# A graph transformer kernel on one core: ScalarE makes the keys' mask addends that GpSimd made, and GpSimd masks three steps of four instead of two

## What is computed

```
qkv = layer_norm(x, g1, be1) @ w_qkv          # 4096 x 3 x 8 heads x 16
scores = einsum("nhd,mhd->hnm", q, k) * 16 ** -0.5
scores = where(adj != 0, scores, -inf)
attn = softmax(scores, axis=-1)
x = x + einsum("hnm,mhd->nhd", attn, v) @ w_proj + b_proj
x = x + gelu(layer_norm(x, g2, be2) @ w1 + b1) @ w2 + b2
```

## Time and profile before

| | us |
|---|---|
| median of 3 runs | 3656.32 |
| lowest, highest | 3652.48, 3665.82 |
| the profiled execution | 3654.05 |
| its span, first to last instruction | 3652.3 |
| layer 0 attention, step 0's exponential to the barrier | 203.6 to 1722 |
| even passes 2 to 12 of layer 0, each | 97.2 to 97.8 |
| odd passes 1 to 13 of layer 0, each | 93.6 to 95.4 |

### The profile page before, as it was taken

One profiled execution on the slowest core, in us unless ns is written; L12 is line 12 of the kernel. 1 busy time (PEld: TensorE's weight loads), 2 busy tenths in 40 slices (PEclk: granted clock), 3 DMA queues, 4 the chain that ended last, 5 costly groups with the idle time before them and its releaser, 6 DMA issues.

```text
span 3652.3 us, 68569 instructions
## 1 busy us (share of the span) xinstructions
PE 3436.8 (94%) x22572; PEld 1388.6 (38%) x22572; DVE 2968.7 (81%) x8997; ACT 2337.5 (64%) x2596; POOL 2489.9 (68%) x1476
## 2 busy tenths in 40 slices
PE   6999999999999999998869999999999999999988
PEld 3443333333333333332634433333333333333326
DVE  6889888888988898870568998999999989999604
ACT  4348686877777777866341466666666666666753
POOL 1057878787878787878110587787888787878870
PEclk9589999999999999999896799999999999999989
DMA  3578787878786869683232546454555555555432
GB/s 131 179 225 261 239 267 226 274 227 281 218 285 210 290 211 295 200 254 94 78 113 84 176 140 187 141 175 154 171 163 169 162 164 165 161 171 157 145 96 67
DMA packets 480351, 676.31 MB, mean 185 GB/s; under 512 B 51552, under 2 KB 272864, under 8 KB 475616
## 3 DMA queue, kind: packets, MB, share of 16 engines
q1 hardware_dynamic: 479568, 671.83, 59.2%
q10 hardware_dynamic: 432, 0.10, 0.0%
HBM read 508.14 MB, written 165.68 MB: 184 GB/s over the span
## 4 chain that ended last, share of the span: by engine, by line
PE 41%; POOL 36%; issue 13%; DVE 7%; DMA 2%; POOLq 1%; ACT 1%; DVEq 0%; SPq 0%; ACTq 0%
POOL arena L929 36%; PE PS L463 13%; PE PS L443 10%; PE PS L476 7%; PE PS L470 7%; DVE spill L806 5%; PE PS L416 3%; POOLq L907 1%; PE PS L449 1%; DVE arena L766 0%; PE PS L586 0%; DMA arena<-out_dram 0%; PE PS L407 0%; ACT o_sb L679 0%; DMA mask<-in_adj_t 0%
## 5 line engine op out<-in xcount | busy, mean ns | idle before, releaser
L806 DVE CUSTOM_DVE_ANT_0 spill<-PS,mask_n 128x512 bf16<-128x512 f32 x4096 | 2635.8, 688 | 278.0 <-PE PS L443 177.4
L671 ACT ACTIVATE arena<-PS 128x1024 f32<-128x1024 f32 x2048 | 1991.8, 1022 | 911.3 <-PE PS L476 870.4
L929 POOL TENSOR_TENSOR arena<-arena,mask 128x1024 int32<-128x1024 int32 x896 | 2136.8, 2385 | 638.0 <-ACT arena L671 633.0
L443 PE MATMUL PS<-k_t,q_t 48*128 48x512 f32 x4096 | 1288.3, 547 | 60.1 <-DVE pmax L806 40.2
L463 PE MATMUL PS<-arena,v_sb 128*32 128x512 f32 x8192 | 1099.4, 609 | 41.6 <-ACT o_sb L679 37.5
L470 PE MATMUL PS<-q_t,k_t 50*128 50x512 f32 x4096 | 934.3, 466 | 0.3 <-POOL arena L919 0.2
L443 PEld LDWEIGHTS PS<-k_t,q_t 48*128 48x128 f32 x4096 | 545.6, 194 | 1022.9 <-DVE pmax L806 911.8
L476 PE MATMUL PS<-arena,idb 64*128 64x512 bf16 x4312 | 841.8, 391 | 0.0
L470 PEld LDWEIGHTS PS<-q_t,k_t 50*128 50x128 f32 x4096 | 400.1, 188 | 199.6 <-ACT arena L671 121.7
L476 PEld LDWEIGHTS PS<-arena,idb 64*128 64x128 bf16 x4312 | 208.9, 95 | 465.5 <-issue 343.3
L806 DVE DVE_READ_ACCUMULATOR2_ANT pmax<- 128x1 f32 x4096 | 340.0, 83 | 0.0
(11 more groups left out here) (54 smaller groups left out, 979.9 us busy)
## 6 DMA issues: line engine op xcount, KB each, us to landing
mask<-m_dram SPq DMA_DIRECT2D x768, 256.0 KB, 2.7
mask_n<-mn_dram SPq DMA_DIRECT2D x768, 128.0 KB, 2.7
adj_in<-in_adj SPq DMA_DIRECT2D x256, 256.0 KB, 3.9
mask<-in_adj_t SPq DMA_DIRECT2D x256, 256.0 KB, 4.0
m_dram<-mask SPq DMA_DIRECT2D x256, 256.0 KB, 3.6
mn_dram<-mask_n SPq DMA_DIRECT2D x256, 128.0 KB, 3.8
mt_dram<-arena SPq DMA_DIRECT2D x256, 128.0 KB, 3.5
arena<-mt_dram SPq DMA_DIRECT2D x256, 128.0 KB, 2.8
```

Of the source, the lines that this page charges most:

```text
L443: pe.matmul(bank, q_t[r0:r0 + KROWS, gb % Q_SLOTS, pair, q * P:(q + 1) * P], k_t[r0:r0 + KROWS, pair, mb * TILE:(mb + 1) * TILE], start=Tr ...
L671: nc.scalar.activation(p_buf[:, t % P_SLOTS, 2 * half:2 * half + 2, :], ps_b[:, 2 * half:2 * half + 2, :], ACT.Exp, scale=SCALE).then_inc( ...
L806: dve.tensor_tensor_reduce(spill[:, j % A_BANKS, :], ps_a[:, j % A_BANKS, :], mask_n[:, v % N_SLOTS, :], 1.0, LOWEST, ALU.subtract, ALU.ma ...
L929: pool.tensor_tensor(p, p, m, ALU.mult).then_inc(p_masked, 1)
```

## The change

POOL's `make_masks` keeps only the 0/1 words. The addends are now made by ACT, in a new function `mask_keys(t)`, from POOL's words: `exp(69 + MASKED * word)`, written to `mask_t` as bf16. The value is positive, so the identity matrix `idb` becomes its negative. ACT's stream has `mask_keys(t + 2)` right behind the second exponential of step t, and ahead of any `mask_rows` there. And `pooled` in layer 0's even passes now holds for three steps of four (all but t % 4 == 0) instead of two.

```
         def pooled(L, t):
 
-            return L > 0 or t // MT % 2 == 1 or t % 2 == 1
+            return L > 0 or t // MT % 2 == 1 or t % 4 > 0
...
+            def mask_keys(t):
+                nb, s, slot = t // (2 * MT), t % MT, t % M_SLOTS
+                act.wait_ge(mask01_made, MADE[t + 1])
+                if nb > 0:
+                    act.wait_ge(b_scored, 2 * (t - MT) + 2)
+                    if s == 0:
+                        act.wait_ge(mt_stored, nb * MT * 16)
+                nc.scalar.activation(mask_t[:, s, :], mask01[:, slot, :].bitcast(U32), ACT.Exp,
+                                     bias=far[:], scale=MASKED).then_inc(t_made, 1)
...
+                for t in range(2):
+                    if made(L, t):
+                        mask_keys(t)
                 for t in range(STEPS):
                     exp_pair(L, t, 0)
                     if t > LAG and t % MT == LAG:
                         keep_o(L, t // MT - 1)
                     exp_pair(L, t, 1)
-                    while made < len(visits) and visit_step(visits[made]) - 3 < t + 1:
-                        mask_rows(visits[made])
-                        made += 1
+                    if t + 2 < STEPS and made(L, t + 2):
+                        mask_keys(t + 2)
+                    while at < len(visits) and visit_step(visits[at]) - 3 < t + 1:
+                        mask_rows(visits[at])
+                        at += 1
                 keep_o(L, 2 * NB - 1)
...
             def make_masks(t):
-                nb, s, slot = t // (2 * MT), t % MT, t % M_SLOTS
+                slot = t % M_SLOTS
                 m = mask01[:, slot, :]
                 pool.wait_ge(adjt_loaded[slot], fills(0, t) * 16)
                 pool.tensor_scalar(m, m.bitcast(U32), 1.0, 0.0, ALU.min, ALU.max).then_inc(mask01_made, 1)
-                if nb > 0:
-                    pool.wait_ge(b_scored, 2 * (t - MT) + 2)
-                    if s == 0:
-                        pool.wait_ge(mt_stored, nb * MT * 16)
-                pool.wait_ge(mask01_made, MADE[t + 1])
-                pool.tensor_scalar(mask_t[:, s, :], m, -MASKED, MASKED, ALU.mult, ALU.add).then_inc(t_made, 1)
...
-    ident = give("ident", np.eye(P, dtype=ml_dtypes.bfloat16))
+    ident = give("ident", -np.eye(P, dtype=ml_dtypes.bfloat16))
```

More of the change, by code:

```diff
@@ L689, in mask_rows @@
                                      bias=far[:], scale=MASKED).then_inc(n_made, 1)
+            def mask_keys(t):
[7 more added lines that the diff above has]
+                                     bias=far[:], scale=MASKED).then_inc(t_made, 1)
             def attend(L):
                 visits = [v for v in range(NV) if rows_made(L, v)]
-                made = 0
-                while made < len(visits) and visit_step(visits[made]) < 3:
-                    mask_rows(visits[made])
-                    made += 1
+                at = 0
+                while at < len(visits) and visit_step(visits[at]) < 3:
+                    mask_rows(visits[at])
[3 more added lines that the diff above has]
+                        mask_keys(t)
                 for t in range(STEPS):
```

## The result

| | before | after |
|---|---|---|
| median, us (5 runs each on one chip) | 3656.38 | 3691.47 |
| lowest, highest | 3652.48, 3665.82 | 3678.69, 3696.44 |
| the profiled execution, its span | 3654.05, 3652.3 | 3685.58, 3683.7 |
| odd passes 1 to 13 of layer 0 | 93.6 to 95.4 | 93.5 to 95.5 |
| even passes 2 to 12 of layer 0 | 97.2 to 97.8 | 101.5 to 104.4 |

A forecast was written before the change was run, and what follows sets the result against it. A ring between ACT and PE was taken as the bound. Terms 6.4 + 2.1 - 2.2 + 7.0 + 9.6 = +22.9 us gave 3679 us beside 3656.32, range 3656 to 3704.

The forecast's parts named there:

- The ring: Middle of even passes: ACT's addends wait for POOL's words behind products, 0.16 us lost per four-step cycle, +6.4 us.
- the gain of 0.27 a step: Even passes: each step moved to POOL saves 0.27 us, 64 steps 17.3 us if nothing else were late.
- Starts of passes: Pass starts: ACT's wait for words, 7 x 0.3 = +2.1 us, against saved steps worth -2.2 us.
- the saved step: First steps of a pass: ACT's wait hides in PE's long gaps; 8 x -0.27 = -2.2 us.
- Row masks: Pass ends: next pass's first row masks stand behind ACT's addends, delaying exponentials of steps 25 and 27; +7.0 us.
- Late loads: Mid-pass: queries' 1 MB load makes POOL's words late and ACT now waits; 7 x 1.37 = +9.6 us.
- The turn: Pass end after step 27: PE's long gap of 2.08 us hides the remaining delay; costed at nothing.
- Rival 4: Even passes: PE, held more often, drops to its 1.2 GHz clock; adds 12 us, 3691 in all; 12%.
- SP's queue: SP's store waits for ACT's addends with the next words' load behind it; costed at nothing, some 2 us in hand.
- rival 3: SP falls behind, so POOL gets its words late in every cycle; +34 us on the forecast, 3713; 10%.
- Rival 1: Even passes: the whole gain of 17.3 us comes, as POOL's words arrive in time; 3639 us; 8%.
- The signs: Profile after: L698 idle over 10 us, even passes 99 to 101 us, four steps 11.7 to 11.9, products 3.05 apart.

The follow-up runs named there:

- e1: The changed kernel with POOL's words made three steps ahead instead of two, their loads unmoved: 3710.03 us, ratio 1.0142 to the kernel before.
- e7: Changed kernel with queries' load issued earlier, turn as four reductions, words made three steps ahead and their loads one step earlier: 3597.86 us, ratio 0.9828.
- e9: The changed kernel, but step 26 of even passes not masked by POOL (8 products fewer): 3668.67 us, ratio 1.0021.
- e2: The changed kernel with SP's 1 MB load of the next queries issued 20 steps earlier, in an odd pass: 3681.73 us, ratio 1.0054.
- e3: The changed kernel with POOL masking two steps of four as before, so only ACT's addends are new: 3671.03 us, ratio 1.0031.
- e5: The kernel before with DVE's four small turn operations written as four reductions, one drain fewer: 3611.85 us, ratio 0.9865.

## Why the prediction was right, and where it failed

- **The ring.** Right in kind: L698 waits for POOL in three steps of four, and more than half of the gain of 0.27 a step is gone (with the words early, e1 and e7, four steps take 11.33); e1 shows that the words' place in POOL's stream does it. Its size and sign were off: -0.12 a cycle for +0.16. The term at fault is product and words together, 3.05 from the pitch of two unlike operations in the earlier trace rows (2.35 + 0.70). The rows of after have 415.32 to 415.89, 0.57, for words followed by a product, so 2.93. Over the two further steps in which POOL is behind this takes 0.24 off, where the cycle was 0.27 too long; the rest are small terms of both signs, as the latency from the words to ACT (415.96 - 415.93 = 0.03 for 0.08), the addend to the exponential (0.63 for 0.61) and the exponentials (1.92 for 1.94).
- **Starts of passes.** Both terms were too large, and by luck they cancel. The gap before a pass's first step grew by 0.1, from 0.88 to 0.98, and not by 0.3; and the saved step, -0.27 in each pass, isn't there: the gaps before steps 1 to 6 are the same in both traces in the seven later passes, 1.3, 1.4 and 1.7 first, set by the mask turn. The first pass's 4.3 us are the clock's earlier rise, which no term had and the change didn't cause.
- **Row masks.** 1.62 and 1.57 at steps 25 and 27 against the forecast 1.70 and 1.6: +7.0 was forecast, +6.9 measured for these gaps. The part called hidden shows at step 30 (1.72 for 1.11), and is paid for by a shorter turn where that is undisturbed (1.57 + 1.40 in e9, 1.10 + 2.1 or so before). In e1, where the words are there early, the same row masks cost nothing (1.11 and 1.11), so this term hangs on the ring.
- **Late loads.** The mechanism was right, and e2 shows the 1 MB load as its cause. The term was 1.37 a pass from pass 2's load; it measured 1.1 to 2.9, in all 12.6 for 9.6, and the stretches at 1.2 GHz behind it came on top, 17.2 in the table. The load comes later than in the trace it was read from. SP issues the words of step 84 at 443.08 us, 0.55 after the start of step 80's exponentials where it was 0.08, because its store of the addends now waits for ACT; in the other six passes it is 0.55 to 1.52 where it was 0.06 to 0.26. And in pass 2 POOL starts 9.65 us after that issue, before 8.69, for which no run shows the cause; in the other passes that time is at most 0.1 longer than before.
- **The turn: the step that failed.** "After step 27 PE's turn leaves a long gap [...], which hides the rest". The turn was taken as slack at no cost, and what DVE does in it wasn't looked at, although the diff makes step 26, whose product runs then, a POOL step. The sign was in the trace of before: a cast of 1.00 us in odd passes and of some 0.18 in even ones. The row measured +17.9 for 0, and e9 puts the price at 20 us, more than the whole shortfall of 12: the cycle and the first steps, 12 us better than forecast in the table, hid a part of it.
- **The clock: an alternative that was an addition.** Rival 4 was given 12% and a time of its own, 3691, the measured one to the microsecond. This is luck in part: the rest of the forecast was to hold beside it, and it didn't. The rival should have hung on the waits that the sum itself had put at PE: who forecasts 1.4 us more idle time in seven places, behind which PE is full of work, has to price the slower microseconds behind them as well. The five executions of after agree: the shortest, 3678.69 us, has a mean granted clock of 0.951, the longest, 3696.44, of 0.947.
- **SP's queue.** Its waits for the addends rose from 50.2 us to 123.2, which the prediction cost at nothing. POOL's waits for loads fell from 29 to 20, so rival 3 did not happen; but the 0.5 us and more by which the loads are issued later is part of the late load's price. The nearest relative of rival 3 is e1, where POOL ran ahead of the loads.
- **Rival 1** failed as argued. The Trainium skill's rule of taking work off GpSimd (Perfetto Trace Analysis, Optimizing GPSIMD Operations) did not hold in e3, which does only that (1.0031), and came true only in e7, behind four other edits.
- **The signs.** L698's idle time, the gap of over 2 us in mid-pass and the unchanged odd passes came. Even passes of 101.5 to 104.4 us for 99 to 101, four steps in 11.50 for 11.7 to 11.9 and products 2.93 apart for 3.05 did not.

The table's parts don't split exactly into waits and clock. Cast and subtraction make 8 x 1.0 + 2.2 = 10 us, the late gaps 12.6, the row masks 6.9; eleven more stretches in even passes at 1.5 us would make 16, and the cycle and first steps -8, of which 4.3 are the clock in pass 0. The sum is 38 for 34.7 measured; that an idle turn hides a part of each is likely, and not shown.

## What to carry to other kernels

When a change gives GpSimd more steps, list the small VectorE operations on the critical path that will now run beside a GpSimd operation, and look in the trace for the same line at two durations: a wait of this kind stands inside the row, with no idle time before it. When an engine gets a wait for another engine's product, ask in every queue how early its inputs are there, and move the producer and its loads by the same step: here the producer alone made the kernel slower (e1, 1.0142), and with its loads moved too, beside the queries' load moved and the turn as reductions, it was faster (e7). And count what follows a new idle time of PE, not only the idle time. Last, compare traces stretch by stretch also where nothing should differ: 4.3 us of this comparison were the clock's rise at the start.

## What the runs showed of the hardware that was not expected

- A VectorE cast or copy of 128x16 fp32 elements takes 0.18 us alone; started while a GpSimd operation runs it lasts until that one's end, up to 1.19 us here, and a two-input subtraction of that size 2.41. It waits for GpSimd's 0.61 us operation as well (the copy of 0.52 that ends at 481.35 beside words that end at 481.30). Reductions of the same size, in the same place, never did: 0.18 to 0.19 us in 32 of 32, 28 of them beside a GpSimd operation. Writing four tiny operations as reductions gave 1.35% of the whole kernel.
- PE's clock fell to 1.2 GHz for 3.4 us (now and then 6.8), 14 times in a layer instead of 2, behind idle times of PE of 1.3 to 2.6 us and one of 4.92 in the traces of before and after. Removing one such place moved some of the stretches to another, idle by no more than before (e2), so a stretch can't be charged to one wait alone. Which idle times are followed by one is left open. Of the seven late loads the two without one have the shortest, 0.76 and 1.07 us (the others 1.27 to 2.56); but of the first seven even turns, at 1.84 to 1.87 each, two have none, and of odd turns at 1.37 some have one and some not. In e5, where PE idles 0.46 to 0.73 us at the turns of passes 0 to 13, there is none.
- From the start of a GpSimd operation of 0.61 us it is 0.57 to the start of a product behind it and 0.6 to one of its own kind, but in the earlier trace rows 0.77 to the one that reads its result, and 0.70 from that to the next words: who takes such distances from rows has to take the pair, not the operation.
